# Placing GpSimd's down-weight sums between the LayerNorm scales of the next batch

## The reference

```python
x = x + _layernorm(_L0_attn_ref(_layernorm(x), Wq, Wk, Wv, Wo))
x = x + _layernorm(_L0_ffn_ref(_layernorm(x), gate_cp, up_cp, down_cp))

# attention over features: q, k, v = x Wq, x Wk, x Wv, each transposed to (512, S)
scores = einsum('bes,bfs->bef', qT, kT) / sqrt(HEAD_DIM)      # 512 x 512 for each batch
out = (softmax(scores) @ vT) transposed, @ Wo

# feed-forward: weights of 2048 x 512 come from a cubic spline over few control points
gate_w, up_w, down_w = spline_reconstruct(gate_cp), spline_reconstruct(up_cp), spline_reconstruct(down_cp)
out = (silu(h gate_w^T) * (h up_w^T)) down_w^T
```

## Time and profile before

| | us |
|---|---|
| median of 3 runs (872.71 to 875.8) | 875.4 |
| the profiled execution, its own time | 878.51 |
| its span, first to last instruction | 876.6 |
| PE busy | 764.5 (87%) |
| DVE busy | 525.6 (60%) |
| ACT busy | 369.9 (42%) |
| POOL busy | 446.5 (51%) |
| mean granted TensorE clock | 0.931 |

### The profile page before, as it was taken

How to read it: one execution, slowest core, us unless ns; L and a number is a source line. 1 busy time by engine, 2 the same in 40 slices (tenths; PEclk the granted TensorE clock), 3 DMA queues, 4 the chain that set the end, 5 groups by cost and what they waited for, 6 DMA issues and landing times.

```text
span 876.6 us, 19208 instructions
## 1 busy us (share of the span) xinstructions
PE 764.5 (87%) x7152; PEld 514.7 (59%) x7152; DVE 525.6 (60%) x1025; ACT 369.9 (42%) x632; POOL 446.5 (51%) x616
## 2 busy tenths in 40 slices
PE   5696899999999998998485999979879799798996
PEld 3574667786778776776232555645546456464565
DVE  6562853685368534656364667757567577673553
ACT  3330333243234322323354646646456465564641
POOL 4399449744974487014143444544445355354542
PEclk9798799999999999899587998989989899898998
DMA  8345347513751375118706053262542623516122
GB/s 295 127 157 165 106 132 241 170 48 124 249 170 48 121 251 131 33 45 273 257 13 228 3 172 131 90 213 74 164 139 74 210 92 119 171 59 220 49 63 73
DMA packets 64313, 120.54 MB, mean 138 GB/s; under 512 B 12144, under 2 KB 28656, under 8 KB 62192
## 3 DMA queue, kind: packets, MB, share of 16 engines
q1 hardware_dynamic: 64240, 119.53, 41.4%
HBM read 82.94 MB, written 36.57 MB: 136 GB/s over the span
## 4 chain that ended last, share of the span: by engine, by line
PE 26%; SPq 10%; DMA 5%; DVE 4%; ACT 3%; issue 3%; POOL 0%; ACTq 0%; DVEq 0%
SPq L885 8%; PE gbank L1401 5%; PE ubank L1401 4%; PE ybank L1440 3%; DMA token_features<-z_lo 3%; PE ybank L1442 2%; PE ybank L1441 2%; PE mbank L1415 2%; DMA out<-x_res 1%; ACT gated L1237 1%; PE turned L960 1%; PE ybank L1429 1%; DVE inter L1304 1%; ACT act L1233 1%; PE ybank L1431 1%
## 5 line engine op out<-in xcount | busy, mean ns | idle before, releaser
L1192 POOL TENSOR_TENSOR act<-inter,act 128x512 f16<-128x512 f32 x128 | 158.2, 1245 | 177.2 <-ACT act L1233 177.2
L1304 DVE SCALAR_TENSOR_TENSOR inter<-ubank,c_up,gated 128x512 f32<-128x512 f32 x128 | 95.9, 749 | 91.4 <-ACT gated L1237 86.6
L1440 PE MATMUL ybank<-down,act 128*128 128x160 f16 x512 | 112.8, 239 | 0.0
L1441 PE MATMUL ybank<-down,act 128*128 128x160 f16 x512 | 112.2, 238 | 0.0
L1442 PE MATMUL ybank<-down,act 128*128 128x160 f16 x512 | 112.2, 238 | 0.0
L1237 ACT ACTIVATE gated<-gbank,c_gate 128x512 f32<-128x512 f32 x128 | 87.8, 686 | 57.7 <-PE gbank L1401 57.6
L1233 ACT CAST act<-inter 128x512 f16<-128x512 f32 x128 | 78.9, 616 | 47.4 <-DVE inter L1304 47.4
L1401 PE MATMUL gbank<-z,s_twice 128*32 128x512 f16 x512 | 55.1, 421 | 44.8 <-ACT gated L1237 29.6
L1440 PEld LDWEIGHTS ybank<-down,act 128*128 128x128 f16 x512 | 50.9, 99 | 41.8 <-issue 38.0
L1401 PEld LDWEIGHTS gbank<-z,s_twice 128*32 128x32 f16 x512 | 13.3, 94 | 73.4 <-ACT gated L1237 35.7
L1401 PE MATMUL ubank<-z,s_twice 128*32 128x512 f16 x512 | 53.7, 410 | 2.5 <-DVE inter L1304 2.5
(11 more groups left out here) (190 smaller groups left out, 2111.8 us busy)
## 6 DMA issues: line engine op xcount, KB each, us to landing
x_ln<-x SPq DMA_DIRECT2D x64, 256.0 KB, 3.4
z<-token_features SPq DMA_DIRECT2D x16, 1024.0 KB, 6.2
job<-job_in SPq DMA_DIRECT2D x24, 640.0 KB, 5.2
shared<-x SPq DMA_DIRECT2D x32, 256.0 KB, 2.7
x<-shared SPq DMA_DIRECT2D x32, 256.0 KB, 2.0
token_features<-z_hi SPq DMA_DIRECT2D x64, 128.0 KB
token_features<-z_lo SPq DMA_DIRECT2D x64, 128.0 KB
x_res<-x SPq DMA_DIRECT2D x32, 256.0 KB, 2.7
```

The source lines that it names most:

```text
L1192: pool.tensor_tensor(hidden[par][:, i, TOK:2 * TOK], inter[:, i % INTERS, :], hidden[par][:, i, 0:TOK], ALU.subtract).then_inc(inter_ready, 1)
L1304: dve.scalar_tensor_tensor(out=inter[:, i % INTERS, :], in0=ubank[:], scalar=c_up[:], in1=gated[:, i % 2, :], op0=ALU.mult, op1=ALU.mult). ...
L1440: pe.matmul(out, hidden[par][:, r, high], box[:, 0], start=False, stop=False)
L1441: pe.matmul(out, hidden[par][:, r, high], box[:, 1], start=False, stop=False)
```

## The change

In the bodies of batches 0 to 2 (`more` True), GpSimd's order becomes: unit chunk 0, sum 0, sum 1, unit chunk 1, and then the eight `ln_scale`, with half a sum behind each: the multiplication of sum 2 behind tile 0, the two additions of sum 2 behind tile 1, the multiplication of sum 3 behind tile 2, and so on to the additions of sum 5 behind tile 7. The body of batch 3 keeps its order. On SyncE, `store_units` 0 goes ahead of jobs 2 and 3, and jobs 4 and 5 go in between and behind the loads of token tiles 4 to 7. The count of operations and of transfers stays what it was.

```diff
@@ block.sync, body @@
-                load_job(b, 2)
-                load_job(b, 3)
+                if not more:
+                    load_job(b, 2)
+                    load_job(b, 3)
                 store_units(2 * b, True)
-                load_job(b, 4)
-                load_job(b, 5)
+                if more:
+                    load_job(b, 2)
+                    load_job(b, 3)
+                else:
+                    load_job(b, 4)
+                    load_job(b, 5)
                 store_units(2 * b + 1, more)
                 if more:
+                    load_x(b + 1, XR)
+                    load_x(b + 1, XR + 1)
+                    load_job(b, 4)
+                    load_x(b + 1, XR + 2)
+                    load_x(b + 1, XR + 3)
+                    load_job(b, 5)
                     load_job(b + 1, 0)
                     load_job(b + 1, 1)
-                if more:
-                    for t in range(XR, NT):
-                        load_x(b + 1, t)
                 else:
...
@@ block.gpsimd @@
-            def sum_job(b, k):
-
-                done, free = held(pool, b * JOBS + k + 1), held(pool, b * JOBS + k + 1)
-                loads = held(pool, (b * (JOBS // 2) + k // 2 + 1) * 16)
-                pool.wait_ge(job_loaded[k % 2], loads)
+            def multiply_job(b, k):
+
+                pool.wait_ge(job_loaded[k % 2], held(pool, (b * (JOBS // 2) + k // 2 + 1) * 16))
                 pool.tensor_tensor(job[:, k % 2, 0], job[:, k % 2, 0], job[:, k % 2, 1], ALU.mult).then_inc(job_mult, 1)
+
+            def add_job(b, k):
+
+                done = held(pool, b * JOBS + k + 1)
                 pool.wait_ge(job_mult, done)
                 pool.tensor_tensor(job[:, k % 2, 0, 0:2], job[:, k % 2, 0, 0:2], job[:, k % 2, 0, 2:4],
                                    ALU.add).then_inc(job_add, 1)
                 pool.wait_ge(job_add, done)
-                pool.wait_ge(job_ready, free)
+                pool.wait_ge(job_ready, done)
                 pool.tensor_tensor(sums[:, k], job[:, k % 2, 0, 0], job[:, k % 2, 0, 1], ALU.add).then_inc(job_summed, 1)

+            def sum_job(b, k):
+                multiply_job(b, k)
+                add_job(b, k)
+
             def body(b, more):
-                for c in range(2):
-                    sum_job(b, 2 * c)
-                    sum_job(b, 2 * c + 1)
-                    unit_weights(2 * b + c)
-                sum_job(b, 4)
-                sum_job(b, 5)
                 if more:
+                    unit_weights(2 * b)
+                    sum_job(b, 0)
+                    sum_job(b, 1)
+                    unit_weights(2 * b + 1)
                     for t in range(NT):
                         ln_scale(b + 1, t)
+                        if t % 2 == 0:
+                            multiply_job(b, 2 + t // 2)
+                        else:
+                            add_job(b, 2 + t // 2)
                 else:
+                    for c in range(2):
+                        sum_job(b, 2 * c)
+                        sum_job(b, 2 * c + 1)
+                        unit_weights(2 * b + c)
+                    sum_job(b, 4)
+                    sum_job(b, 5)
                     for m in range(XR):
                         feats.scale(pool, m)
```

## The result

| | before | changed |
|---|---|---|
| median, us | 874.06 (4 runs) | 861.91 (860.83 to 864.76, 4 runs) |
| ratio | | 0.987, interval 0.983 to 0.991 |
| profiled execution, its own time | 878.51 | 862.21 |
| its span | 876.6 | 860.4 |
| mean granted clock | 0.931 | 0.943 |

The ratio is 11.5 us less. In a later job, where the changed kernel ran again beside the kernel before, it had 864.49 against 873.32 and a ratio of 0.990, interval 0.986 to 0.993, that is 9.2 us less. The forecast was 10.7 us and 864.7, in a range of 860 to 870; of the 2.8 us between 864.7 and 861.91, 1.3 are that the kernel before had 874.06 this time, not 875.4.

What follows compares the result with a forecast made beforehand. VectorE's 14.42 us wait for GpSimd's scale held batch 0; the matmul engine bounds Wo and Wv in batches 1 and 2. -13.3 + 1.7 + 0.9 = -10.7 us, from 875.4 to 864.7, range 860.0 to 870.0.

Steps and rivals of the forecast that it cites:

- Part 1: Batch 0: VectorE's wait for GpSimd's first scale goes and the Wv stage runs as in batch 1; gain 13.30 us.
- the walk: Stepping GpSimd's new order from 50.59 in batch 0: first scale at about 75.7, softmax's last low part at about 72.0.
- Part 2: Softmax of batch 0: GpSimd's long operations lengthen VectorE's L590 and L593, last parts ready at about 72.0; cost 1.7 us.
- Moving the Wo stage as a whole: Batch 0: the softmax's 1.7 us delay was to shift the entire Wo stage.
- Part 3: Half sums between the scales, batches 0 to 2: lengthened L527 pushes the first y statistics by 0.3 us each, 0.9 together.
- the choice between its own row and its siblings: L527's row, never lengthened, gave 863.8; siblings L590 and L593, lengthened beside GpSimd, gave 864.7 and were followed.
- The rule of the Trainium skill: VectorE operations in two-port mode or with two SBUF inputs contend with GpSimd; the first issued holds the shared port throughout.
- Part 4: Transfers and queues: job loads arrive in time, put at nothing, with 3.0 us a batch as upper end.

Runs made afterwards that it cites:

- whole_sums: Changed kernel with the interleaving undone: sums 2 to 5 whole ahead of the eight scales, jobs 4 and 5 loaded ahead of token tiles 4 to 7; 880.87 us.
- late_tiles: Changed kernel with SyncE issuing the loads of jobs 4 and 5 ahead of token tiles 4 to 7; 886.72 us in one run.
- changed_again: The changed kernel once more, unaltered, in a later job; 864.49 us.
- small_halves: Changed kernel with the operations of sums 2 to 5 in batches 0 to 2 cut to one column, their sums not computed; 863.25 us.
- double_product: Changed kernel with one more unused 128x640 product behind each of the four multiplications between the scales; 876.55 us in one run.
- last_scale_first: Changed kernel with the first token scale of batch 3 put ahead of sums 4 and 5; 858.87 us, ratio to the kernel before 0.983.
- early tiles: Token tiles 0 to 3 of batch 1 loaded ahead of SyncE's wait for the weight split: in the kernel before 876.88 us, in the changed one 864.92 us.
- chunk_behind_y: last_scale_first with unit chunk 1 of batches 0 to 2 behind the y scales, in batch 3 behind the first token scale; 863.14 us.
- clear_softmax: Changed kernel with sums 0 and 1 and unit chunk 1 of batches 0 to 2 cut to one column, results not computed; 856.87 us in one run.
- chunk_and_early_tiles: chunk_behind_y with token tiles 0 to 3 of batch 1 loaded ahead of the wait for the weight split; 857.37 us, ratio to the kernel before 0.982.
- early_tiles_and_sum: Changed kernel with early tiles, sum 0 of batch 0 ahead of the weight split, those of batches 1 to 3 behind the previous y scales; 865.81 us.

## Why the prediction was right

Part 1, -13.3: right to the hundredth. The Wv stage fell from 24.18 to 10.88, and the first scale was done at 75.69 where the walk had 75.7. whole_sums shows that the new order by itself costs and that the interleaving is needed; late_tiles, that it needs SyncE's new order too.

Part 2, +1.7: the walk was right. The last low part was ready at 71.99 against 72.0, and at 71.87 to 72.60 in the six other executions that have this order of GpSimd up to there (changed_again, small_halves, late_tiles, double_product, whole_sums, last_scale_first). How much of it reaches the Wv stage is less sure. In the first pair of profiles it is 0.71: from the last wait on, the Wo stage took 11.55 us before and 10.59 after. The granted clock stood at 0.50 until 75.90 before and until 75.53 after, so 5.5 and 3.5 us of this ran at the half clock, and half of that difference is the 1.0. But nothing ties this 1.0 to the change: in the six other executions the clock came back between 75.64 and 78.47, and the Wv stage started 0.76 to 2.37 us later than in the kernel before, of which this stretch is known from a single profile. The 1.7 lies inside that. "Moving the Wo stage as a whole" left the clock out; the 1.0 that the first profile is better is luck. The statement that batches 1 and 2 are past this work ahead of the softmax holds for the changed kernel.

Part 3, +0.9: 0.33 and 0.18 measured in the step distances of two batches, where I had 0.3 each. The path is the one told: the first y statistics come 3.44 us behind the start of the y stage (96.95 against 93.51), where it was 2.92 in batch 1 before. small_halves takes exactly this away. The third batch's part can't be told from the variation of the stretch ahead of batch 3. That L527 would be lengthened was the choice between its own row and its siblings: its median rose from 530 to 654 ns, and the first one of batch 0 took 1.69, more than the 1.0 expected, but the evacuation behind it still had 0.51 us of waiting for ScalarE. The rule of the Trainium skill ("SBUF — State Buffer", section "Who interferes with whom") decided rightly here, and the tails of 0.28 and 0.55 us behind GpSimd's operation are the size that the runs add to it.

Part 4, nothing: right, there is no wait of GpSimd for a job transfer in the changed kernel. But that holds for the order chosen: with jobs 4 and 5 ahead of the tiles, late_tiles was 25 us slower.

The sum to the Wv stage of batch 2 was -11.0 (-13.3 + 1.7 + 0.6). It is -12.08 in the first profile, -11.27 in changed_again and -10.33 in last_scale_first, which is the same kernel up to there. The two measured ratios, 11.5 and 9.2 us, lie on both sides of the 10.7 forecast. Their intervals, 8.3 to 14.8 and 6.3 to 12.1 us, are too wide to bear out a single term; the stage starts do that.

What stays open: whether the distance from batch 2 to batch 3 is really 1 us shorter in the changed kernel, and what moves the moment at which the clock comes back in batch 0.

## What to carry to other kernels

When an engine's queue holds a short operation that another engine waits for behind long ones that nobody waits for, split the long ones and put them behind the short one, and reorder the loads with them. Then price the new neighbours: in these runs a long GpSimd operation delayed those VectorE operations with two operands from SBUF, or of the tensor_scalar kind, that met it, and in the softmax of one batch this cost 6.6 us, beside the 13.3 that the change won. And a cure for one of two late things can show nothing until the other is cured, as the early tiles did; run both together before either is given up.

## What the runs showed of the hardware

- A VectorE tensor_scalar (0.49 to 0.55 alone) that begins while a GpSimd tensor_tensor runs ends 0.28 to 0.29 us behind its end, where its own length doesn't reach further; a scalar_tensor_tensor with two SBUF operands (0.66 to 0.75 alone) ends 0.55 behind. The GpSimd operation that follows is then longer, by up to 0.43: a multiplication in the softmax of the kernel before took 1.99 instead of 1.56.
- The granted clock in the softmax of batch 0, beside the matmul engine's waits there: with 1.19, 2.62 and 0.81 us (before) it fell to 0.50 at 69.1 and rose at 75.9; with 2.40, 2.46 and 0.90 (changed) it fell at 65.3 and rose at 75.5; with 0.49, 1.19, 1.46 and 1.58 (chunk_behind_y) it fell at 69.9 and rose at 73.3. With 1.03 and 0.43 (clear_softmax) and with 0.82, 1.19 and 0.42 (chunk_and_early_tiles) it stayed at 1.00.
- Behind the reduction across partitions GpSimd's first tensor_tensor started at 38.26 to 39.51 whichever it was (38.26 in early_tiles_and_sum, 39.28 in the changed kernel, 39.51 in the kernel before), 6.9 or 10.3 us after the end of the operation ahead of it. The cause isn't known from these runs.
